# Routing with one-hot rows built column by column, token numbers multiplied inside the comparison

## What is computed

```
logits = rms_normed(layernorm(x)) * router_scale / sqrt(512) @ router_logits   # (4096, 8)
_, choices = top_2(logits)                        # two experts for each token
xs_order = choices.ravel().argsort()              # the 8192 (token, choice) pairs, by expert
xs_indices = repeat(arange(4096), 2)[xs_order]
sorted_xs = x_flat[xs_indices, :]
gate_out = ragged_dot(sorted_xs, w_gate, tokens_per_expert)
...
out = expert_outputs[xs_reverse_argsort] weighted by the two routing weights
```

## Time and profile before

| | us |
|---|---|
| median of 3 runs | 4832.13 |
| lowest and highest | 4829.42, 4833.49 |
| profiled execution, own time | 4831.27 |
| its span | 4829.6 |
| TensorE busy | 4626.9 |
| VectorE busy | 2897.6 |
| POOL busy | 2258.1 |
| ScalarE busy | 2107.7 |

### The profile page before, as it was taken

The page is one execution under the profiler, slowest core; times in us unless marked ns, Lnnn a source line. Parts: engine busy times, 40 slices in busy tenths (PEclk is TensorE's granted clock), DMA queues, the critical chain, the costliest instruction groups (busy, mean ns, idle before and its releaser), DMA issues. The chain is left out here.

```text
span 4829.6 us, 82831 instructions
## 1 busy us (share of the span) xinstructions
PE 4626.9 (96%) x27966; PEld 3477.5 (72%) x27967; DVE 2897.6 (60%) x5285; ACT 2107.7 (44%) x4111; POOL 2258.1 (47%) x1724
## 2 busy tenths in 40 slices
PE   6999996999999999999998799999899999999999
PEld 4788885666666666666656578888788877778888
DVE  6222225799999999999974722333455548754444
ACT  4222223456676666776662422222322235533222
POOL 1545433278888888888881154543111007500000
PEclk8999998999999999999999799999999999999999
DMA  7233326757777777777764733433522112250110
GB/s 220 83 93 98 93 83 213 260 104 146 148 146 147 146 146 147 147 147 147 146 135 155 231 94 122 131 119 110 179 66 70 55 51 82 70 196 27 35 35 27
DMA packets 245975, 585.69 MB, mean 121 GB/s; under 512 B 30816, under 2 KB 85088, under 8 KB 221152
## 3 DMA queue, kind: packets, MB, share of 16 engines
q0 software_dynamic: 62064, 317.23, 29.2%
q1 hardware_dynamic: 183536, 263.86, 16.7%
HBM read 263.27 MB, written 121.63 MB: 80 GB/s over the span
## 5 line engine op out<-in xcount | busy, mean ns | idle before, releaser
L1373 POOL TENSOR_TENSOR attend_pairs<-attend_pt 128x1024 f32<-128x1024 f32 x512 | 1259.0, 2478 | 197.4 <-ACT attend_pt L1338 197.2
L1386 DVE TENSOR_REDUCE attend_mx<-attend_am_ps 128x1 f32<-128x512 f32 x2048 | 1251.0, 678 | 124.7 <-PE attend_am_ps L1246 121.4
L1338 ACT ACTIVATE attend_pt<-attend_sc_ps 128x512 f32<-128x512 f32 x2048 | 1039.9, 618 | 285.3 <-PE attend_sc_ps L1234 285.1
L1246 PE MATMUL attend_am_ps<-attention_kst,attend_qst 96*128 96x512 f32 x2048 | 859.1, 425 | 10.2 <-DMA attend_qst<-q_parts 10.1
L1234 PE MATMUL attend_sc_ps<-attend_qst,attention_kst 98*128 98x512 f32 x2048 | 816.7, 400 | 1.5 <-ACT attend_pt L1338 1.3
L1637 PE MATMUL ffn_gu_ps<-ffn_y_hi,ffn_w 128*128 128x512 f32 (+1 forms) x1584 | 568.8, 369 | 3.5 <-DVE ffn_y_lo L1767 3.0
L1637 PE MATMUL ffn_gu_ps<-ffn_y_lo,ffn_w 128*128 128x512 f32 (+1 forms) x1584 | 569.0, 369 | 0.0
L1246 PEld LDWEIGHTS attend_am_ps<-attention_kst,attend_qst 96*128 96x128 f32 x2048 | 392.8, 192 | 239.8 <-DVE attend_mx L1386 122.8
L1260 PE MATMUL attend_pv_ps<-attend_pt,attention_v 128*32 128x256 f32 x8192 | 497.6, 384 | 0.0
L741 DVE TENSOR_TENSOR expert_ac<-expert_gu_ps,expert_gl 128x512 f32<-128x512 f32 x142 | 98.1, 691 | 640.5 <-ACT expert_gl L698 640.5
L1234 PEld LDWEIGHTS attend_sc_ps<-attend_qst,attention_kst 98*128 98x128 f32 x2048 | 389.4, 190 | 88.7 <-ACT attend_pt L1338 11.7
(11 more groups left out here) (329 smaller groups left out, 7725.6 us busy)
## 6 DMA issues: line engine op xcount, KB each, us to landing
attend_pairs<-attend_pairs POOLq DMA_DIRECT2D x189, 1024.0 KB, 7.4
weights_raw<-experts_dram POOLq DMA_DIRECT2D x76, 512.0 KB, 4.1
ys<-expert_ob SPq DMA_DIRECT2D x142, 256.0 KB, 2.2
attend_qst<-q_parts SPq DMA_DIRECT2D x192, 128.0 KB, 3.9
yn<-route_yb SPq DMA_DIRECT2D x64, 256.0 KB, 4.1
ffn_xb<-x SPq DMA_DIRECT2D x64, 256.0 KB, 2.9
keyvalue_xb<-x SPq DMA_DIRECT2D x64, 256.0 KB, 2.8
weights_lo<-experts_dram SPq DMA_DIRECT2D x24, 512.0 KB, 9.5
```

The lines of the kernel that those rows point to most:

```text
L1246: pe.matmul(am[:, bank, :], qst[0:KROWS, n % 2, h * HALF + hd, :], kst[0:KROWS, o:o + 4 * P], start=True, stop=True).then_inc(am_rdy, 1)
L1338: act.activation(pt[:, u % RING, g * 4 * P:(g + 1) * 4 * P], sc[:, s % SBANKS, :], ACT.Exp, scale=HD ** -0.5).then_inc(p_rdy, 1)
L1373: pool.tensor_tensor(pairs[:, slot(half, j), :], pt[:, 2 * p % RING, :], pt[:, (2 * p + 1) % RING, :], ALU.add).then_inc(pair_rdy, 1)
L1386: dve.tensor_reduce(mx[:, hh, block:block + 1], am[:, am_slot["max", a] % MBANKS, :], AX.X, ALU.max).then_inc(mx_rdy, 1)
```

## The change

Each column is now made by two `tensor_scalar` operations with a single tensor source, the constant numbers 0 to 127 or 0 to 71. The value that is compared, and for `in_tile` the token number as a factor in the same instruction, are operands of one number per partition. The semaphore `tile_rdy` and its wait are gone. The semaphores for TensorE rise once for eight columns, as before.

```diff
             def hot(n):
-                q = slice(n * HOT, (n + 1) * HOT)
-                dve.tensor_tensor(in_tile[:, q, :], spread(tilef[:, q], SLOT_TILES), spread(iota_tile[:], HOT, 1), ALU.is_equal).then_inc(tile_rdy, 1)
-                dve.tensor_tensor(in_row[:, q, :], spread(rowf[:, q], P), spread(iota_row[:], HOT, 1), ALU.is_equal).then_inc(row_rdy, 1)
-                dve.wait_ge(tile_rdy, n + 1)
-                dve.tensor_tensor(in_tile[:, q, :], in_tile[:, q, :].bitcast(F32), spread(token[:, q], SLOT_TILES), ALU.mult).then_inc(token_rdy, 1)
+                for q in range(n * HOT, (n + 1) * HOT):
+                    a = dve.tensor_scalar(in_row[:, q, :], iota_row[:], rowf[:, q:q + 1], None, ALU.is_equal)
+                    b = dve.tensor_scalar(in_tile[:, q, :], iota_tile[:], tilef[:, q:q + 1], token[:, q:q + 1], ALU.is_equal, ALU.mult)
+                a.then_inc(row_rdy, 1)
+                b.then_inc(token_rdy, 1)
```

More of the change, by code:

```diff
@@ L181, in routing_stage @@
             mem.sem(n) for n in ("bn_rdy", "mv_rdy", "sd_rdy", "rstd_rdy", "y_rdy", "tr_rdy", "yT_rdy", "lgT_rdy", "lgT_kept", "lg_rdy"))
-        step_done, msd_rdy, gap_rdy, egap_rdy, both_rdy, summed, totals_rdy, ranked, tile_rdy, token_rdy, row_rdy, rows_rdy, tab_rdy, turned = (
+        step_done, msd_rdy, gap_rdy, egap_rdy, both_rdy, summed, totals_rdy, ranked, token_rdy, row_rdy, rows_rdy, tab_rdy, turned = (
             mem.sem(n) for n in ("step_done", "msd_rdy", "gap_rdy", "egap_rdy", "both_rdy", "summed", "totals_rdy", "ranked",
-                                 "tile_rdy", "token_rdy", "row_rdy", "rows_rdy", "tab_rdy", "turned"))
+                                 "token_rdy", "row_rdy", "rows_rdy", "tab_rdy", "turned"))
         block = ctx.enter_context(nc.Block())
```

## The result

| | before | after |
|---|---|---|
| median of 7 runs, us | 4826.79 | 4844.28 |
| lowest and highest | 4825.47, 4833.49 | 4841.93, 4853.35 |
| ratio to before | | 1.0032, 95% interval 1.0022 to 1.0041 |
| profiled execution's span | 4829.6 | 4842.1 |

The change makes the kernel slower by 0.32% (4826.79 x 0.0032 = 15.4 us; by the interval 10.6 to 19.8 us). The two medians themselves lie 17.5 us apart, 0.36%, which is inside the interval. Seven runs put the median of before 5 us lower than the three on which the prediction rested.

The account below looks back on a forecast made before the run. VectorE's comparisons were taken to bound both routing stages; 0.1975 + 0.234 us a column made 55.23 us against 39.58, so 4832.13 + 15.65 = 4847.8 us, with an 8-in-10 range of 4841 to 4862.

Parts of the forecast that it names:

- What bounds the stretch: Routing stage, run twice: VectorE's comparisons set the pace, 19.79 us a stage, and a longer run delays everything behind one for one.
- in_row at 0.1975 us a column: New one-source comparison of 128 elements with one per-partition operand, start to start, taken from L2280 of the same shape.
- in_tile at 0.234: New compare-and-multiply of 72 elements with two per-partition operands: 0.234 us a column, from L385's 0.46 us less 0.229.
- The sum for both stages +15.65 us: Both routing stages' comparisons: 55.23 us in place of 39.58, at 0.4315 us a column against 0.309.
- TensorE's clock at nothing, at most 2 us a stage: Start of the expert stage: a later clock rise costs nothing, at most 2 us a stage, and the same to the good.
- Rival 1: New VectorE operations run one element at a time, from equality or fp32r output: +29.0 us, 4861.2 us; chance 0.17.
- rivals 2 and 3: Rival 2: new operations' per-partition operands hidden under the operation ahead, -10.1 us, 4822.0 us, chance 0.06; Rival 3 has its own line.
- Rival 3: in_tile's second operand free, another 0.06 us hidden between alternating forms: 0.364 us a column, +7.0 us, 4839.1 us; chance 0.07.
- The formula for cycles: Skill page's 58 + elements / acceleration cycles for VectorE: a group falls from 2.45 to 1.80 us, both stages save 10.4 us.
- POOL idle near 20 us: Sign in the changed profile: POOL idle before the expert stage near 20 us instead of 11.83.
- Rival 4: POOL's transfer issues in the routing stretch slow VectorE's operations: 2.7 us a stage, +21.0 us in all, 4853.1 us; chance 0.05.
- POOL and the DMA queues get no new work: Routing stage, work beside VectorE's comparisons: the change adds nothing to POOL or the DMA queues; no cost was counted.

## Why the prediction was right

- What bounds the stretch: VectorE alone, nothing beside it as late. Right. The expert stage starts 6.40 us later: 7.29 us of longer stretch less 0.89 us by which the first comparison came earlier.
- in_row at 0.1975 us a column: 0.195 measured. in_tile at 0.234: 0.226, somewhat less than L385 let expect; why was not looked for. (By the prediction's own terms the value is 0.46 - 0.229 = 0.231, not 0.234, and the sum +15.3 us.) A group at 3.45 us: 3.38. The sum for both stages +15.65 us: 14.5 us in the groups.
- The time: +15.65 us forecast, ratio 1.0032; measured 1.0032 (1.0022 to 1.0041). That the ratio fits this well is luck within the interval. The absolute 4847.8 us is 3.5 us above the measured median, mostly because before itself came out 5 us lower.
- TensorE's clock at nothing, at most 2 us a stage: behind the first stage the rest up to the second took 2622.10 us against 2622.22, so nothing there. Behind the second, the expert stage was 4.5 us shorter in this one execution, and no run tells whether the clock has a part in that.
- Rival 1 is refuted by 0.241 us a column without operands, rivals 2 and 3 by the 0.060 us of each operand. Rival 3 was priced wrongly: its 0.364 us a column takes off one of the two savings that it names; with both it is 0.304 us, or 0.7 us less than before in place of 7.0 more.
- The formula for cycles on the Trainium skill's page "VectorE: DVE Perf Modes", section "The TRN2 errata — SBUF-src ops pay a fixed extra latency per instruction", which made the change a gain, has no term for per-partition operands, and this term decides: 3 x 0.060 x 128 = 23 us. Without it, and with POOL unharmed, the stretches would be 8.7 us shorter than before ((22.04 - 17.68) x 2).
- POOL idle near 20 us: 17.47 and 19.02. In the first stage its last issue came 14.2 us behind the first comparison, before 12.8.
- Rival 4 had POOL slowing VectorE. VectorE's distances didn't move; the harm goes the other way, and the line "POOL and the DMA queues get no new work" passed over it. In the changed kernel it is 0.3 us at most for an issue, in a branch with 17 us to spare; with immediates it turned the 8.7 us that VectorE gained into 11.8 us lost over the two stages. No step of the prediction looked for this.

## What to carry to other kernels

Count a one-source VectorE operation start to start as 0.06 to 0.07 us, plus 0.06 us for each per-partition operand, plus 0.52 ns an element, and one with two tensor sources as 0.07 to 0.08 us plus 1.03 ns an element. By these numbers (an estimate; no run has columns of that size) a two-source operation over eight columns beats eight one-source operations with one such operand as long as a column has fewer than about 215 elements ((0.12 - 0.07 / 8) us / 0.52 ns). Before moving or shortening VectorE work beside POOL, ask what of it will hold POOL up: fast one-source operations without operands stopped POOL's transfer issues here for as long as they ran, the same with one operand in every second of them stopped an issue for 10 and 13 us, and two-source ones stopped its tensor operations. And when a stand-in kernel computes wrong numbers, count its instructions before its time is read: here one more tile of expert work cost 9.7 us.

## What the runs showed that was not expected

- A run of 111 short VectorE operations, started 0.10 to 0.14 us apart, starved POOL for 13.6 us as if it were one instruction. In the rows there is no gap between them: each starts before the one ahead has ended.
- In the changed kernel the durations of in_row's operations in the rows rise from 0.27 us at 96.07 us to 0.33 at the end of hot(7) while the distance of their starts stays at 0.42 us for a pair. Durations alone would have shown a slowing that isn't there. The cause was not looked for.
